# State-space stage: adding weighted states by an accumulating transfer in place of GpSimd

## What is computed

```
xc = silu(conv(xm) + conv_b);  dt, Bm, Cm = split(xc @ W_xproj.T)
delta = softplus(dt @ W_dt.T + b_dt);  A = -exp(A_log)
dA = exp(delta[..., None] * A)
dBx = delta[..., None] * Bm[:, :, None, :] * xc[..., None]
def step(h, t):
    h = dA_t * h + dBx_t
    return h, einsum('ben,bn->be', h, C_t)      # sum over the 16 states n
y = (ys + D_skip * xc) * silu(z);  out = y @ W_out.T
```

## Time and profile before

| | us |
|---|---|
| median of 3 runs | 2458.88 (2457.44 to 2459.68) |
| the profiled execution | 2460.9 |
| its span, first to last instruction | 2459.2 |
| the loop of the state-space stage, some | 92 to 1126 (1034) |
| one unit of it | 129.8 |

### The profile page before, as it was taken

One profiled execution on the slowest core, in us unless ns is written; L12 is line 12 of the kernel. 1 busy time (PEld: TensorE's weight loads), 2 busy tenths in 40 slices (PEclk: granted clock), 3 DMA queues, 4 the chain that ended last, 5 costly groups with the idle time before them and its releaser, 6 DMA issues. The chain is left out here.

```text
span 2459.2 us, 35798 instructions
## 1 busy us (share of the span) xinstructions
PE 1911.8 (78%) x10252; PEld 1465.2 (60%) x10253; DVE 1678.1 (68%) x3193; ACT 1184.7 (48%) x2021; POOL 1515.8 (62%) x1152
## 2 busy tenths in 40 slices
PE   6787879686979787875599999907877784799970
PEld 2445455554555454544499999904655664699970
DVE  1779898989989898985644444437634897644438
ACT  2677777777777767773232222226632441111112
POOL 1799999999999999994133333335622420355532
PEclk9888979798989888887699999958988896799995
DMA  3111111111101011112411111142000014122226
GB/s 123 38 35 40 39 37 36 39 39 37 39 23 52 27 49 31 43 36 77 165 48 47 47 48 48 41 139 77 9 18 11 9 35 163 42 71 70 70 65 192
DMA packets 76780, 138.63 MB, mean 56 GB/s; under 512 B 10369, under 2 KB 47873, under 8 KB 75858
## 3 DMA queue, kind: packets, MB, share of 16 engines
q1 hardware_dynamic: 62994, 99.67, 12.4%
q0 software_dynamic: 13632, 37.24, 4.8%
HBM read 104.86 MB, written 32.01 MB: 56 GB/s over the span
## 5 line engine op out<-in xcount | busy, mean ns | idle before, releaser
L787 DVE TENSOR_TENSOR_SCAN a_hs<-a_dA,a_carry,a_hs 128x512 f32<-128x512 f32 x512 | 628.3, 1264 | 63.5 <-ACT a_dA L559 53.7
L399 POOL TENSOR_TENSOR a_hs<-a_u,a_b_bc 128x1024 f32<-128x1024 f32 (+1 forms) x292 | 634.9, 2182 | 2.3 <-POOL a_u L381 1.9
L929 PE MATMUL a_h_ps<-k_ident,a_hs 128*128 128x128 f32 x2064 | 328.3, 308 | 174.7 <-DVE a_acc L750 95.6
L929 PEld LDWEIGHTS a_h_ps<-k_ident,a_hs 128*128 128x128 f32 x2064 | 268.4, 158 | 293.5 <-DVE a_hs L787 86.2
L559 ACT ACTIVATE a_dA<-a_delta,a_a_neg 128x512 f32<-128x512 f32 x512 | 350.1, 687 | 39.6 <-DVE a_hs L787 38.4
L411 POOL TENSOR_TENSOR a_acc<-a_acc,a_part 128x512 f32<-128x512 f32 x242 | 331.7, 1371 | 28.6 <-ACT a_part L573 28.3
L573 ACT ACTIVATE a_part<-a_h_ps,a_c_tok 128x512 f32<-128x512 f32 x242 | 166.0, 686 | 203.8 <-PE a_h_ps L929 176.0
L1229 POOL DMA_INDIRECT expert_rows<-m0e_ys,k_pair x71 | 78.7, 1109 | 232.5 <-DVE m0e_ys L1285 221.6
L750 DVE SCALAR_TENSOR_TENSOR a_acc<-a_h_ps,a_c_tok,a_acc 128x512 f32<-128x512 f32 x242 | 176.3, 728 | 46.5 <-PE a_h_ps L929 46.4
L863 PE MATMUL a_fx<-a_hT,a_w_x 128*128 128x512 f32 x432 | 200.9, 597 | 2.2 <-ACT a_halo L495 1.4
L1295 DVE TENSOR_TENSOR m0e_hT<-m0e_gs,m0e_u 128x512 f32<-128x512 f32 x70 | 48.2, 688 | 191.5 <-ACT m0e_gs L1248 191.5
(11 more groups left out here) (420 smaller groups left out, 3793.2 us busy)
## 6 DMA issues: line engine op xcount, KB each, us to landing
a_b_bc<-b_rows SPq DMA_DIRECT2D x132, 256.0 KB, 3.2
c_y<-expert_rows SPq DMA_DIRECT2D x16, 512.0 KB, 5.6
q_y<-expert_rows SPq DMA_DIRECT2D x16, 512.0 KB, 5.9
norm_rows<-a_x SPq DMA_DIRECT2D x9, 512.0 KB, 3.3
m0w_up<-in_m_up SPq DMA_DIRECT2D x1, 4096.0 KB, 12.1
m0w_gate<-in_m_gate SPq DMA_DIRECT2D x1, 4096.0 KB, 22.2
m0w_down<-in_m_down SPq DMA_DIRECT2D x1, 4096.0 KB, 32.1
c_xl<-in_L_attn_x SPq DMA_DIRECT2D x8, 512.0 KB, 3.7
```

What stands on the lines that cost most here:

```text
L399: last = pool.tensor_tensor(hs[k][:, w, :], u[s][:, w, :], b_bc[:, k:k + 1, :].broadcast_to([P, width, T]), ALU.mult)
L787: dve.tensor_tensor_scan(hs[k][:, c, :], dA[c][:], hs[k][:, c, :], carry[:, hf, c, n:n + 1], ALU.mult, ALU.add).then_inc(s_scan, 1)
L929: last = pe.transpose(hT_ps[j % 2][:, c * P:(c + 1) * P], hs[(n - 1) % NBUF][:, c, j * P:(j + 1) * P], ident[:])
```

## The change

The sums of tiles 1 and 3 are no longer POOL instructions. Once per iteration (not in iteration 1) POOL issues one transfer from `part` to `acc` that adds to its target, 128 partitions x 2 tiles x 512 floats, 512 KB. It waits first for both parts of this iteration (`s_part`) and for the landing of the transfer before (`s_add`, now counted in sixteens). `part` holds two sets, used by even and odd iterations, so ACT waits, once per iteration ahead of tile 1, for the transfer of two iterations ago. A landed transfer is also what `y0` and the final `output` wait for.

Around it: ahead of the loop POOL clears `part`, then issues two such transfers of zeros and waits for each before it goes on. To make room, `hn` and `x1` become one buffer. ACT must therefore not write `hn` in iteration 1 before the store of the rows from `x1` has landed: the wait for `s_rst` moves from iteration 14 to iteration 1.

```diff
-        hn = m.sb("hn", [P, TJ, D])
...
         x1 = m.sb("x1", [P, TJ, D])
+        hn = x1
...
-        part = m.sb("part", [P, TJ // 2, ED])
+        part = m.sb("part", [P, 2, TJ // 2, ED])
...
-        ND, NO, ADDS = len(ON), len(OFF), len(OFF) * (NS - 1)
+        ND, NO, ADDS = len(ON), len(OFF), NS - 1
...
+        def added_count(U, n, back=0):
+
+            return lin(U, 16 * ADDS, 16 * ((n - 1 if n > 1 else 0) + 3 - back))
...
             pool.memset(z[1][:], 0.0).then_inc(s_prep, 1)
-            pool.memset(acc[1][:], 0.0).then_inc(s_prep, 1)
+            pool.memset(acc[1][:], 0.0).then_inc(s_const, 1)
             pool.memset(xc[1][:], 0.0).then_inc(s_prep, 1)
-            pool.sem_inc(s_add, NO)
-            pool.wait_ge(s_const, 2)
+            pool.memset(part[:], 0.0).then_inc(s_const, 1)
+            pool.wait_ge(s_const, 4)
+            pool.sem_inc(s_prep, 1)
+            for k in range(2):
+                pool.dma_start(acc[1][:, OFF[0]:TJ:2, :], part[:, k], accum_op=ALU.add).then_inc(s_add, 16)
+                pool.wait_ge(s_add, 16 * (k + 1))
...
-            def add(U, n, j, s):
-
-                if j not in OFF or n == 1:
+            def add(U, n, s):
+
+                if n == 1:
                     return
-                pool.wait_ge(s_part, part_count(U, n, j))
-                if n == 0:
-                    pool.wait_ge(s_add, added_count(U, 0, j) + -NO)
-                elif n > 2:
-                    pool.wait_ge(s_add, added_count(U, n - 1, j))
-                pool.tensor_tensor(acc[s][:, j, :], acc[s][:, j, :], part[:, j // 2, :], ALU.add).then_inc(s_add, 1)
+                pool.wait_ge(s_part, part_count(U, n, OFF[-1]))
+                pool.wait_ge(s_add, added_count(U, n, 1))
+                pool.sem_inc(s_go, 1)
+                pool.dma_start(acc[s][:, OFF[0]:TJ:2, :], part[:, n % 2], accum_op=ALU.add).then_inc(s_add, 16)
...
                         for q in range(2):
                             product(U, ahead, q, hf if ahead < NS else 1 - hf)
-                            add(U, n, 2 * q + 1, hf if n else 1 - hf)
+                        add(U, n, hf if n else 1 - hf)
...
-                    act.wait_ge(s_add, added_count(U, 0, j) + -NO if n == 0 else added_count(U, n - 1, j))
-                    to = part[:, j // 2, :]
+                    if j == OFF[0]:
+                        act.wait_ge(s_add, added_count(U, n - 2) if n > 3 else added_count(U, 0, (2, None, 0, 1)[n]))
+                    to = part[:, n % 2, j // 2, :]
...
                         if n == 1:
+                            act.wait_ge(s_rst, lin(U, 16, 16))
                             act.wait_ge(s_pw, lin(F, 1, 1))
                         if n == 14:
                             for o in ("o0", "o1"):
                                 act.wait_ge(s_free[side(o)], count(o, U))
-                            act.wait_ge(s_rst, lin(U, 16, 16))
...
                         pe.wait_ge(s_acc, lin(U, NS * ND, 2 * ND))
-                        pe.wait_ge(s_add, lin(U, ADDS, 2 * NO))
+                        pe.wait_ge(s_add, added_count(U, 0))
```

More of the change, by code:

```diff
@@ L225, in mamba_phase @@
         s_part = m.sem("weighted_by_act")
-        s_add = m.sem("summed_by_pool")
+        s_add = m.sem("summed_by_transfers")
+        s_go = m.sem("ready_to_sum")
         s_carry = m.sem("carry")
@@ L286, in part_count @@
             return lin(U, NS * NO, NO * n + OFF.index(j) + 1 + NO)
-        def added_count(U, n, j):
-            return lin(U, ADDS, NO * (n - 1 if n > 1 else 0) + OFF.index(j) + 1 + NO)
+        def added_count(U, n, back=0):
+            return lin(U, 16 * ADDS, 16 * ((n - 1 if n > 1 else 0) + 3 - back))
         ROWS = R + 2 * NS
@@ L450, in _ @@
             end = (0, 2 * NB, None)
-            for j in OFF:
-                add(end, 0, j, 1)
+            add(end, 0, 1)
             rms(TILES - TJ, lambda per_: per_ * (2 * NB + 1))
@@ L954, in _ @@
             pe.wait_ge(s_acc, lin(end, NS * ND, 2 * ND))
-            pe.wait_ge(s_add, lin(end, ADDS, 2 * NO))
+            pe.wait_ge(s_add, added_count(end, 0))
             pe.wait_ge(s_da, 2 * NB * NS * EC + EC)
```

## The result

| | before | after |
|---|---|---|
| median of 4 runs each, us | 2459.28 | 2509.59 (2507.87 to 2512.33) |
| span of the profiled execution | 2459.2 | 2507.7 |
| PE's first turn of the front | 17.25 | 33.56 |
| one unit of the loop, mean of seven | 129.8 | 133.2 |
| last start of `front_power` to PE's last `output` | 124.9 | 136.3 |

The kernel is slower by a factor of 1.0204, 95% interval 1.0186 to 1.0222. The forecast was 2436 us, in a range of 2404 to 2485; it has the wrong sign, and the measured time lies outside the range. The lower rows of the table say where: 14 to 16 us ahead of the loop, 3.4 us in each of the seven full units between two starts of `front_power`, 11 us from the last of these to the end. 14.8 us (first `front_power` of the loop, at 96.50 before and 111.31 after) + 23.6 + 11.4 = 49.8, against 48.5 us in the spans; 1.3 us are won back behind the loop.

What follows compares the result with a forecast made beforehand. POOL was taken as the latest engine by a little, DVE and PE nearly as full, ACT and PE pacing iterations 9 to 12. 2459.2 - 34.4 (loop) + 7.3 (start) + 3.9 (end) = 2436 us, range 2404 to 2485.

Steps and rivals of the forecast that it cites:

- the transfers in the loop: In the loop: each issue takes POOL 0.97 to 1.94 us, the landing comes 5.6 us after it, b_bc loads undisturbed.
- The prediction's other estimate, 4.4 us: Landing time of a 512 KB transfer by the Trainium skill's pages, 2.0 + 2.4 us; would give 2432 in all.
- The rival in which the transfers bound the loop by their own length: Each transfer waits for the one before, so long landings pace the iterations; 2513 us at an 8 us landing; chance 0.18.
- L: Time from a transfer's issue to its landing, taken as 5.6 us everywhere, between 4.0 and 6.6.
- the worth of POOL's relief: In the loop: taking the additions off POOL wins 4.3 us a unit, between 0.7 and 7.7; 34 us in eight units.
- The 0.7 us of the silus: End of iteration 8: ACT's silus start at PE's turn, 534.87, not behind POOL at 535.60; 0.7 us a unit won.
- Ahead of the loop: Before the loop: two start transfers in a row delay PE's first turn; 7.3 us lost, between 4.1 and 9.3.
- Who waits for it: In the loop: landings are covered; state 0's lands at 618.0, before `y0` starts at 619.11, so no loss.
- At the end of the loop: Last part to PE's last output: the last landing is uncovered; 3.9 us lost, between 2.3 and 4.9.
- the softplus: In the loop: DVE's six softplus instructions get 2.7 us a unit shorter, between 0 and 5.3, with POOL's additions gone.
- Nothing is won in the loop: Rival: DVE loses as much to POOL's products in pairs, only the silus gain stays; 2465 us; chance 0.14.
- ACT's wait for `front_power`: In the loop: `front_power` comes earlier and ACT's 13.3 us wait goes; 0.9 us a unit won, between 0 and 1.7.

Runs made afterwards that it cites:

- e12: e2 with two waits that hold POOL's products at states 12 and 13 until DVE's first and second softplus pairs are done: 2432.6 us.
- e1: The changed kernel with the two start transfers cut to 16 columns of one tile and placed behind `front_power`: 2497.6 us.
- e2: e1 with the sums of states 0 and 15 added by POOL itself, states 2 to 14 still by transfer: 2467.8 us.
- e10: The changed kernel with only the two waits that hold POOL's products at states 12 and 13 for DVE's softplus pairs: 2467.5 us.
- e7: e3 with POOL waiting for ACT's part of tile 1 between the two products of an iteration: 2426.6 us; sums incomplete.
- e4: The kernel before with POOL's additions left out and everything else in place: 2432.3 us; sums incomplete.
- e9: e2 with a wait for tile 1's part between products and the two waits for DVE's softplus pairs: 2431.6 us.
- e3: The changed kernel with no transfer at all, semaphores passed on at once: 2461.0 us; sums incomplete.
- e13: e2 with state 11 also summed by POOL: 2466.7 us.

## Why the prediction was wrong

From "after" to e12 are 77.0 us, in three steps, each edit on top of the last: 12.0 (e1), 29.8 (e2), 35.2 (e12). Each undoes a step of the prediction that failed. In another order the shares are others: the waits of e12 alone give 42.1 (e10).

The forecast of 2436.0 and the span of 2507.7 are 71.7 us apart. 7.5 of them lie ahead of the loop (14.8 where 7.3 were said), 3.3 at its end (7.2 for 3.9), and 62 in the eight units, 7.8 in each; 1.3 were won back behind the loop. Of the 7.8 us, 2.5 are the chain of states 15 and 0 (e1 to e2) and 5.1 the products beside the softplus with what hangs on it (e2 to e12).

That e12's 2432.6 lies close to the forecast's 2436 is in part luck. The forecast had 34.4 us won in the loop and 11.2 lost at start and end. e12 has two waits that the changed kernel lacks, pays hardly anything at start and end (0.7 us later into the loop, "end" 1.9 us shorter), and is 26.7 us faster than "before" in the median.

- **Right: the transfers in the loop.** Issue 1.21 us, landing 5.4 us in the median; b_bc undisturbed. The prediction's other estimate, 4.4 us, was a microsecond short. The rival in which the transfers bound the loop by their own length (L of 7.1 or more) did not occur: POOL waits 26.9 us in all for landings, and e12 with 104 transfers of 512 KB has units as long as e7 with none (125.9 and 125.8). No engine is seen to be slowed by DMA that is busy for 0.45 of the time.
- **Right: the worth of POOL's relief.** Forecast 4.3 us a unit, unit "125 to 126 us"; e4 has 125.7, e9 and e12 125.9. It needs that POOL's products do not run against the softplus, and the changed kernel does not see to that. The 0.7 us of the silus were not measured apart; in the one unit looked at, ACT's last part ahead of them waits for PE (0.54 us) and no longer for POOL.
- **Wrong, "Ahead of the loop": 7.3 us, measured 16.3** at PE's first turn, 12.0 in the median. It took one L of 5.6 us for every place. Two landings were to take 11.2 us and took 19.4 (10.4 and 9.0), in a stretch where the DMA engines are busy all the time; even 8 KB take 6.6 there. The rows from which L was made are medians over the whole program, and no row was read of how long a load takes while all inputs are being loaded.
- **Wrong, "Who waits for it": "it is covered by 1.1 us".** The step took state 0's transfer to go out as soon as its part was ready. It left out what stands ahead of it on POOL: two products and then the landing of state 15, which the same paragraph names as POOL's wait and which takes 6.8 to 7.6 us there. In the unit shown the issue comes 4.5 us behind the part (505.86, 510.34), and the issues of 15 and 0 stand 8.05 us apart. Price 2.5 us a unit.
- **Wrong, "At the end of the loop": 3.9 us, measured 7.2.** The same omission: the issue waits 3.8 us for state 15's landing (1171.0 to 1174.8), and then comes the landing that was counted, 8.9 us from the last part to PE where it was 1.8.
- **Wrong, the softplus, and the largest: a gain of 2.7 us a unit, measured a loss of 1.4** (13.8 for 12.4). The prediction saw that POOL's products would run in pairs, put it into a rival ("Nothing is won in the loop", 0.14), and priced the forecast with "POOL stands idle for part of it". It did not ask *where* POOL would be let go: one wait for both parts holds it back until just before the softplus, and then lets all products go at once. With an issue ahead of them they also keep DVE out until they are done. The rival named the first half of this. Its 2465 holds 11.2 us for start and end; without them it is 2453.6, and e3, which has the products in a row and no transfer, took 2461.0.
- **Wrong, half: ACT's wait for `front_power`.** 0.9 us a unit was to be won; the wait stayed (12.8 for 13.3 us), since `front_power` stands behind the issue of state 0 and its wait. With no summing on POOL at all it goes (2.9 us in e3, 3.2 in e4); e12 has 8.7 us.
- The rivals were priced one at a time; the one on longer transfers had 18 us for start and end, the others 11. The case that came, a longer start and end, a chain at each seam and bursts of products together, was in none of them.

## What to carry to other kernels

When work leaves an engine, ask what its instructions did for the order of the rest: here the waits of the additions made the gaps between products, and one late wait in their place made bursts. These cost as much as the additions had (e3 against e4: 29 us), and more with an issue ahead of them. A transfer that waits for the one before it is a chain; where a unit ends or the loop does, count its links and give the last one to an engine (2.35 us of addition for 5.4 us of landing). Transfers that only set up a count belong behind whatever others wait for.

## What the hardware showed

- DVE instructions with two inputs in SBUF, 1.21 us alone, take up to 5.46 us beside a run of four POOL products and up to 5.90 beside two long ones (e13). If an issue of a transfer stands just ahead of the run, DVE gets in only behind the whole run, of four short or two long products (6.59, 7.54, 6.32 us a pair), and POOL is not slowed (5.40 and 5.12 us). If no issue does, each DVE instruction is held by one POOL instruction at most, and both slow each other (6.99 us for four short products and 3.43 for the pair; 5.65 us for two long ones and 6.12 for the pair). The Trainium skill ("SBUF — State Buffer", SBUF: two separate sides) says that such a DVE instruction and a GpSimd instruction take the shared port as a lock, each for one whole instruction. The rows with no issue ahead agree with that. It does not say who comes next when several GpSimd instructions are queued; in the rows with an issue ahead DVE does not come in between them.
- The instruction that follows an issue on POOL begins 0.77 us after it and is some 0.5 us longer (2.82 against 2.35 us for a product, 2.13 against 1.66 for `front_power`). So is every further product of that run, each starting some 0.5 us before the one ahead has ended; the run as a whole is not longer for it.
- An addition over both tiles in one instruction takes 2.35 us, two of one tile 2 x 1.27 to 1.36.
- An accumulating transfer of 512 KB between two SBUF tiles lands 5.4 us after its issue in the median, in a loop with 95 GB/s in all; 6.8 to 7.6 us where another 512 KB are stored beside it, and 8.9 and 10.1 us at the start, where 300 GB/s are moved.
